# Another order of the deep slots: scores and value products side by side on TensorE

## The chip, the cores and the metric

The kernel runs on 1 core of one Trainium2 chip. The metric is the device time of one execution, in microseconds (us); lower is better. The core has five engines that the text names as the profile does: PE (TensorE matmul; PEld is its weight load), DVE (VectorE), ACT (ScalarE), POOL (GpSimd) and SP (SyncE, which issues the DMAs).

## The reference

Sixteen sequences of 256 tokens, 128 features each, float32:

```
x = x + local_attention(layernorm(x))       # first layer: 16 heads of 8, windows of 32
y = layernorm(x)
for i in range(6):                          # the deep layers
    y = attn(shift(y), Wqkv[i], ...) + y    # 16 heads of 64, windows of 32, look back one window,
                                            # q and k normalised and rotated (rope)
    y = ffn(shift(y), ...) + y              # layernorm, W1 (2 x 341), gate * gelu, W2
x = x + y
```

`shift` moves the second half of the features one token on. The queries, keys and values are products of the tokens with Wqkv (128 x 3072); softmax runs over each query's window and the one before.

## The kernel before, in words

The first layer comes first and takes about a tenth of the time; the change does not touch it. The six deep layers are 96 **instances** (layer x sequence), 16 sequences per layer. Each engine runs a written-out list of steps, its **slot**, over and over (`pe_deep_slot`, `act_deep_slot`, `dve_deep_slot`, `pool_deep_slot`, `sp_deep_slot`). Each step names the instance it works on as an offset: `pe_scores_of(e, s, b, at, 0, 1)` is score pair 1 of the instance of this slot, `pe_project_in(..., 2, 0)` projection 0 of the instance two further on. So several instances are in work at once, and one slot holds the work of one instance. The engines are bound together by semaphores alone: each step waits for the counts that its inputs and its output buffer need, and an engine never goes past a step that waits.

The steps of one instance:

- `pe_project_in` 0 to 7 (L901 to L903): Q and K, each as three bf16 products of 512 columns into one PSUM bank. ACT squares the bank (`act_square`, L1050), DVE sums the squares (`dve_sum_squares`, L1128) and applies rope (`dve_rope`, L1147 and L1148), after which the bank is free. POOL adds the two halves (`pool_rotate`, L1264) and, once the norms are refined (`dve_refine`, L1190 to L1194), scales them (`pool_scale`, L1278). PE transposes (`pe_transpose` 0 to 7, L950), ACT copies the result to q and k (`act_copy_t`, L1070).
- `pe_values_in` 0 to 3: V, the same three products; ACT copies the bank to a stage (`act_copy_v`, L1082), SP's DMAs place it.
- For each of four pairs (128 queries x 8 heads): scores (`pe_scores_of`, mask L967 and products L973, in 64 x 64 tiles of the array), `dve_max_of` (L1203), `dve_shift` (L1215), `act_exp_of` (L1092), `dve_sum_of` (L1228, L1230), `pool_normalise_of` (L1288), `pe_transpose_probs_of` (L989), `act_copy_pt_of` (L1102), the value products (`pe_values_of`, L1008, 96 x 64) and `act_copy_out` (L1114). There is one buffer for scores, one for transposed probabilities and one for outputs.
- `pe_project_out` (L1024), `dve_residual_of` (L1240).
- The FFN: `act_ff_shift` (L1385), `pe_ff_mean` (L1314), `dve_ff_centre` (L1430), `act_ff_square` (L1395), `pe_ff_variance` (L1325), `dve_ff_variance` (L1440), the seed and refine shared with Q and K, `pe_ff_rstd` (L1340), `dve_ff_norm` (L1450), `act_ff_affine` (L1405), `pe_ff_up` in three chunks (L1357), `act_ff_gelu` (L1417, after which ACT loads the exponential's table again, L1420), `dve_ff_gate` (L1462), `pe_ff_down` (L1370), `dve_ff_residual` (L1475). `dve_outer` (L1488) adds the outer residual in the last layer.

**The ring.** Projections, value projections, Q/K transposes, the output projection and the FFN's products share three PSUM banks. `WORK_RING` lists these 27 users in PE's order; the user at place j has bank j mod 3, and before it starts PE waits until the user three places before has been read (`pe_wait_bank`): for `pj` by DVE's rope, for `t` and `v` by ACT's copy, for `mu` by DVE's variance, for `rb` by the norm, for `up` by the gate, for `dn` and `out` by the residuals. Two waits that bear on the FFN and on the buffers:

```
e.wait_ge(s.ff_gated, k.c[NF] + (c - 1))                # act_ff_gelu: GELU c waits for gate c - 2
    if c == NF - 1:
        e.preload_act_table_set(EXP_SET)                # after the last GELU
```

```
e.wait_ge(s.t_full, k.c[8] + (u + 1 - 8))               # pool_rotate u: transpose u of the instance before is done
```

The weights of the next layer are split on POOL during the slots (`pool_next_weights`, six pieces in every layer but the last).

## Time and profile before

| | |
|---|---|
| median of 3 runs | 3563.55 us (3558.95 to 3563.68) |
| the profiled execution | 3559.2 us |
| its span, first to last instruction | 3557.4 us |
| granted clock of TensorE, mean | 0.997 |
| PE busy | 3480.7 us, 98% |
| PEld busy | 2617.2 us, 74% |
| DVE busy | 3220.0 us, 91% |
| ACT busy | 2739.7 us, 77% |
| POOL busy | 2580.3 us, 73% |
| share of PE in the chain that ended last | 96% |
| one slot, from an instance to the next | 33.01 us in 91 of 95 steps |

Busy time is the union of an engine's instructions over the span. The chain is followed back from the last instruction, at each step to what released it. The ends of matmuls are modelled and overlap the next matmul's start, so lengths on PE are best taken from one start to the next. In the timeline below a row is a run of like instructions on one engine: its start, its length, engine, line, operation, output and inputs, their number, and in brackets the idle time before it and what ended it.

### The profile page before, as it was taken

To read this page: it belongs to the slowest core of one execution; us is meant where nothing else is said; L and a number is where in the kernel's file an instruction comes from. 1 tells how busy PE (TensorE), PEld (TensorE's weight loads), DVE (VectorE), ACT (ScalarE), POOL (GpSimd) and SP (SyncE) were. 2 spreads that over 40 slices of the span, in tenths; PEclk is the share of its full clock that TensorE was granted. 3 is DMA by queue.
4 is the path that set the end of the run, shared out by engine and by line. 5 is a ranking of instruction groups with operands and counts; after the bars stand their busy time and mean duration, and the time that the engine had idled before them with its cause. 6 is when DMAs were issued, how large, how long until landed. Compare 5 with 4: busy or idle time off the path is not lost.

```text
span 3557.4 us, 112862 instructions
## 1 busy us (share of the span) xinstructions
PE 3480.7 (98%) x45216; PEld 2617.2 (74%) x45216; DVE 3220.0 (91%) x5488; ACT 2739.7 (77%) x4727; POOL 2580.3 (73%) x2263
## 2 busy tenths in 40 slices
PE   7998899999999999999999999999999999999998
PEld 5776577777777777777777777777777777777776
DVE  6877899999999999999999999999999999999995
ACT  4665677887887887887788788788788878878876
POOL 2433887777778777778777777877877877777772
PEclk9999999999999999999999999999999999999999
DMA  1000222122112212212212221221221221121121
GB/s 44 27 2 29 55 54 57 40 60 55 47 44 57 54 47 55 54 37 57 66 38 51 54 50 44 66 51 39 54 57 37 66 51 41 44 74 49 36 51 41
DMA packets 61573, 171.67 MB, mean 48 GB/s; under 512 B 9472, under 2 KB 21248, under 8 KB 60672
## 3 DMA queue, kind: packets, MB, share of 16 engines
q1 hardware_dynamic: 61056, 164.46, 18.1%
q8 instruction: 363, 5.95, 0.7%
q14 instruction: 154, 1.26, 0.1%
HBM read 21.82 MB, written 4.19 MB: 7 GB/s over the span
## 4 chain that ended last, share of the span: by engine, by line
PE 96%; issue 1%; DVE 1%; ACT 1%; POOL 1%; DVEq 0%; POOLq 0%; ACTq 0%
PE bank L1008 11%; PE bank L950 10%; PE bank L989 10%; PE bank L1024 9%; PE bank L1357 8%; PE bank L901 8%; PE bank L973 7%; PE bank L903 7%; PE bank L902 7%; PE bank L1370 4%; PE bank L967 3%; PE bank L370 2%; PE bank L350 2%; PE bank L1325 1%; PE bank L335 1%; PE bank L1340 1%
## 5 line engine op out<-in xcount | busy, mean ns | idle before, releaser
L1264 POOL TENSOR_TENSOR rotbuf<-mbuf 128x512 f32<-128x512 f32 x768 | 969.0, 1272 | 510.2 <-PE bank L950 321.6
L1278 POOL TENSOR_TENSOR rotbuf<-rotbuf,rs 128x512 f32<-128x512 f32 x768 | 787.0, 1045 | 66.0 <-DVE rs L1194 66.0
L1128 DVE TENSOR_REDUCE ss<-sq 128x8 f32<-128x512 f32 x768 | 516.7, 677 | 156.4 <-ACT sq L1050 156.2
L1288 POOL TENSOR_TENSOR probs<-probs,rden 128x768 f32<-128x768 f32 x384 | 564.6, 1470 | 120.9 <-DVE rden L1230 120.9
L1147 DVE TENSOR_TENSOR mbuf<-bank,table 128x512 f32<-128x512 f32 x768 | 528.5, 688 | 13.4
L1148 DVE TENSOR_TENSOR mbuf<-bank,table 128x512 f32<-128x512 f32 x768 | 523.2, 681 | 0.0
L1050 ACT ACTIVATE sq<-bank 128x512 f32<-128x512 f32 x768 | 458.9, 598 | 53.9 <-PE bank L903 21.9
L1008 PEld LDWEIGHTS bank<-probs_t,vbuf 96*64 96x64 f32 x12288 | 389.4, 138 | 144.4 <-issue 104.3
L1070 ACT ACTIVATE kbuf<-bank 128x512 f32<-128x512 f32 x384 | 217.9, 593 | 347.1 <-PE bank L950 347.1
L950 PE MATMUL bank<-ident,rotbuf 128*128 128x128 f32 x3072 | 451.9, 275 | 15.2 <-DVE mbuf L1148 8.6
L901 PE MATMUL bank<-weights,inputs 128*128 128x512 bf16 x1152 | 442.8, 384 | 10.5 <-DVE mbuf L1148 8.2
L1008 PE MATMUL bank<-probs_t,vbuf 96*64 96x64 f32 x12288 | 442.4, 225 | 1.1 <-ACT outs_t L1114 1.1
L902 PE MATMUL bank<-weights,inputs 128*128 128x512 bf16 x1152 | 438.8, 381 | 0.0
L903 PE MATMUL bank<-weights,inputs 128*128 128x512 bf16 x1152 | 438.6, 381 | 0.0
L950 PEld LDWEIGHTS bank<-ident,rotbuf 128*128 128x128 f32 x3072 | 356.7, 141 | 103.3 <-DVE mbuf L1148 60.3
L989 PE MATMUL bank<-ident,probs 128*96 128x128 f32 x3072 | 404.0, 274 | 0.6 <-ACT probs_t L1102 0.5
L1102 ACT ACTIVATE probs_t<-bank 96x1024 f32<-96x1024 f32 x384 | 390.6, 1017 | 5.0 <-PE bank L989 2.7
L1215 DVE TENSOR_TENSOR probs<-bank,row_max 128x768 f32<-128x768 f32 x384 | 366.8, 955 | 6.7
L989 PEld LDWEIGHTS bank<-ident,probs 128*96 128x96 f32 x3072 | 340.8, 129 | 38.9 <-POOL probs L1288 1.5
L1203 DVE TENSOR_REDUCE row_max<-bank 128x8 f32<-128x768 f32 x384 | 364.7, 950 | 1.3 <-PE bank L973 1.3
L1228 DVE TENSOR_REDUCE den<-probs 128x8 f32<-128x768 f32 x384 | 362.1, 943 | 0.0
L1024 PE MATMUL bank<-outs_t,weights 128*128 128x256 f32 x1536 | 347.6, 379 | 0.6 <-DVE x_stream L1475 0.6
(111 smaller groups left out, 6114.6 us busy)
## 6 DMA issues: line engine op xcount, KB each, us to landing
vbuf<-v_stage SPq DMA_DIRECT2D x192, 384.0 KB, 4.5
vbuf<-v_stage SPq DMA_DIRECT2D x192, 256.0 KB, 4.0
vbuf<-v_stage SPq DMA_DIRECT2D x96, 128.0 KB, 4.5
stage<-in_wqkv SPq DMA_DIRECT2D x36, 256.0 KB, 5.3
weights<-in_wo SPq DMA_DIRECT2D x6, 512.0 KB, 6.8
weights<-in_x_t SPq DMA_DIRECT2D x1, 2048.0 KB, 7.3
out_t<-weights SPq DMA_DIRECT2D x1, 2048.0 KB, 6.3
weights<-out_t SPq DMA_DIRECT2D x1, 2048.0 KB, 10.4
```

Of the source, the lines that this page charges most:

```text
L901: e.matmul(out, xh, wh, start=True, stop=False)
L902: e.matmul(out, xh, wl, start=False, stop=False)
L903: return e.matmul(out, xl, wh, start=False, stop=True)
L950: mm = e.transpose(work_bank(b, "t", u)[:, P * q:P * (q + 1)], b.rot[:, u, P * q:P * (q + 1)], b.ident[:, :])
L989: mm = e.transpose(b.pt[parity][0:BLOCK_K, P * j:P * (j + 1)], b.deep_probs[:, p % 2, 4 * parity + j, :], b.ident[:, :])
L1008: mm = e.matmul(b.out[r, col:col + BLOCK_Q], b.v[:, k.par, 2 * t + blk_half, DIM_HEAD * h:DIM_HEAD * (h + 1)], b.deep_ptf[:, p % 2, 512 * ...
L1024: mm = e.matmul(out, b.wo[k.layer % 2][:, chunk, :], b.ot8[:, chunk, :], start=chunk == 0, stop=chunk == INNER // P - 1)
L1147: e.tensor_tensor(b.m1[:, u % 2, :].rearrange("p (h s d) -> p h s d", h=8, s=2), pj, cos, ALU.mult)
L1148: e.tensor_tensor(b.m2[:, u % 2, :].rearrange("p (h s d) -> p h s d", h=8, s=2), pj[:, :, ::-1, :], sin, ALU.mult).then_inc(s.pj_free, 1)
L1264: e.tensor_tensor(b.rot[:, u, :], b.m1[:, u % 2, :], b.m2[:, u % 2, :], ALU.add).then_inc(s.rotated, 1)
L1278: e.tensor_tensor(v, v, r, ALU.mult).then_inc(s.scaled, 1)
L1288: e.tensor_tensor(probs, probs, b.rden[:, p % 2, :].unsqueeze(2).broadcast_to([P, 8, BLOCK_K]), ALU.mult).then_inc(s.probs, 1)
```

## The change

It writes the four engines' slots and the ring in another order; the steps themselves, their number and their waits are as they were. On PE, `pe_scores_of` and `pe_values_of` stood apart from each other in eight places of a slot. Now they stand in five: values 1 alone, scores 1 with values 2, values 3 with scores 2, scores 3 alone, values 0 with scores 0. Some steps work on another instance than before in the same slot (an offset that is one more or less), among them ff up, projection 5 and value projection 1.

```diff
--- before.py
+++ after.py
@@ -60,10 +60,10 @@
 PAIRS = 4
 WORK_BANKS = 3
 WORK_RING = (
-    ("pj", 5, 1), ("up", 0, -3), ("up", 1, -3), ("up", 2, -3), ("pj", 6, 1), ("mu", 0, -2), ("pj", 7, 1),
-    ("t", 6, 0), ("v", 1, 1), ("t", 7, 0), ("v", 2, 1), ("pj", 0, 2), ("v", 3, 1), ("pj", 1, 2),
-    ("t", 0, 1), ("t", 1, 1), ("rb", 0, -2), ("t", 2, 1), ("dn", 0, -3), ("t", 3, 1), ("pj", 2, 2),
-    ("v", 0, 2), ("pj", 3, 2), ("t", 4, 1), ("out", 0, -1), ("t", 5, 1), ("pj", 4, 2),
+    ("t", 5, 0), ("pj", 6, 1), ("mu", 0, -2), ("pj", 7, 1), ("t", 6, 0), ("t", 7, 0), ("dn", 0, -3),
+    ("v", 2, 1), ("pj", 0, 2), ("v", 3, 1), ("pj", 1, 2), ("t", 0, 1), ("t", 1, 1), ("rb", 0, -2),
+    ("t", 2, 1), ("pj", 2, 2), ("out", 0, -1), ("pj", 3, 2), ("v", 0, 2), ("t", 3, 1), ("pj", 4, 2),
+    ("t", 4, 1), ("pj", 5, 2), ("up", 0, -2), ("up", 1, -2), ("up", 2, -2), ("v", 1, 2),
 )
 PE_REACH = (-3, 2)
 ACT_REACH = (-3, 2)
@@ -1562,141 +1562,138 @@
 
 def pe_deep_slot(e, s, b, at):
 
-    pe_project_in(e, s, b, at, 1, 5)
-    pe_scores_of(e, s, b, at, 0, 0)
-    pe_ff_up(e, s, b, at, -3, 0)
-    pe_values_of(e, s, b, at, -1, 0)
-    pe_ff_up(e, s, b, at, -3, 1)
-    pe_transpose_probs_of(e, s, b, at, -1, 2)
-    pe_ff_up(e, s, b, at, -3, 2)
+    pe_transpose(e, s, b, at, 0, 5)
     pe_project_in(e, s, b, at, 1, 6)
     pe_ff_mean(e, s, b, at, -2)
     pe_values_of(e, s, b, at, -1, 1)
     pe_project_in(e, s, b, at, 1, 7)
+    pe_transpose_probs_of(e, s, b, at, -1, 3)
+    pe_ff_variance(e, s, b, at, -2)
     pe_scores_of(e, s, b, at, 0, 1)
-    pe_ff_variance(e, s, b, at, -2)
-    pe_transpose_probs_of(e, s, b, at, -1, 3)
+    pe_values_of(e, s, b, at, -1, 2)
     pe_transpose(e, s, b, at, 0, 6)
-    pe_values_in(e, s, b, at, 1, 1)
     pe_transpose(e, s, b, at, 0, 7)
+    pe_ff_down(e, s, b, at, -3)
     pe_values_in(e, s, b, at, 1, 2)
     pe_project_in(e, s, b, at, 2, 0)
-    pe_values_of(e, s, b, at, -1, 2)
     pe_values_in(e, s, b, at, 1, 3)
-    pe_scores_of(e, s, b, at, 0, 2)
     pe_project_in(e, s, b, at, 2, 1)
     pe_values_of(e, s, b, at, -1, 3)
-    pe_transpose_probs_of(e, s, b, at, 0, 0)
+    pe_scores_of(e, s, b, at, 0, 2)
     pe_transpose(e, s, b, at, 1, 0)
     pe_transpose(e, s, b, at, 1, 1)
+    pe_transpose_probs_of(e, s, b, at, 0, 0)
     pe_ff_rstd(e, s, b, at, -2)
     pe_transpose(e, s, b, at, 1, 2)
-    pe_ff_down(e, s, b, at, -3)
-    pe_transpose(e, s, b, at, 1, 3)
     pe_project_in(e, s, b, at, 2, 2)
-    pe_transpose_probs_of(e, s, b, at, 0, 1)
+    pe_project_out(e, s, b, at, -1)
+    pe_project_in(e, s, b, at, 2, 3)
     pe_scores_of(e, s, b, at, 0, 3)
     pe_values_in(e, s, b, at, 2, 0)
-    pe_project_in(e, s, b, at, 2, 3)
+    pe_transpose(e, s, b, at, 1, 3)
+    pe_transpose_probs_of(e, s, b, at, 0, 1)
+    pe_project_in(e, s, b, at, 2, 4)
     pe_transpose(e, s, b, at, 1, 4)
-    pe_project_out(e, s, b, at, -1)
-    pe_transpose(e, s, b, at, 1, 5)
-    pe_project_in(e, s, b, at, 2, 4)
+    pe_project_in(e, s, b, at, 2, 5)
+    pe_values_of(e, s, b, at, 0, 0)
+    pe_scores_of(e, s, b, at, 1, 0)
+    pe_ff_up(e, s, b, at, -2, 0)
+    pe_ff_up(e, s, b, at, -2, 1)
+    pe_ff_up(e, s, b, at, -2, 2)
+    pe_transpose_probs_of(e, s, b, at, 0, 2)
+    pe_values_in(e, s, b, at, 2, 1)
 
 
 def act_deep_slot(e, s, b, at):
 
-    act_square(e, s, b, at, 0, 6)
-    act_copy_pt_of(e, s, b, at, -2, 2)
-    act_ff_square(e, s, b, at, -3)
-    act_square(e, s, b, at, 0, 7)
-    act_exp_of(e, s, b, at, -1, 0)
-    act_copy_out(e, s, b, at, -2, 1)
-    act_copy_t(e, s, b, at, -1, 6)
-    act_copy_v(e, s, b, at, 0, 1)
-    act_copy_pt_of(e, s, b, at, -2, 3)
-    act_copy_t(e, s, b, at, -1, 7)
-    act_square(e, s, b, at, 1, 0)
-    act_seed(e, s, b, at, 0)
-    act_copy_out(e, s, b, at, -2, 2)
-    act_copy_v(e, s, b, at, 0, 2)
-    act_copy_v(e, s, b, at, 0, 3)
-    act_exp_of(e, s, b, at, -1, 1)
-    act_square(e, s, b, at, 1, 1)
+    act_copy_out(e, s, b, at, -2, 3)
     act_copy_t(e, s, b, at, 0, 0)
     act_copy_t(e, s, b, at, 0, 1)
+    act_exp_of(e, s, b, at, -1, 1)
     act_copy_pt_of(e, s, b, at, -1, 0)
     act_copy_t(e, s, b, at, 0, 2)
+    act_square(e, s, b, at, 1, 2)
+    act_exp_of(e, s, b, at, -1, 2)
+    act_input_of(e, s, b, at, 2)
+    act_square(e, s, b, at, 1, 3)
+    act_ff_affine(e, s, b, at, -3)
+    act_ff_shift(e, s, b, at, -2)
     act_copy_t(e, s, b, at, 0, 3)
-    act_square(e, s, b, at, 1, 2)
-    act_copy_out(e, s, b, at, -2, 3)
-    act_ff_affine(e, s, b, at, -3)
     act_copy_v(e, s, b, at, 1, 0)
-    act_square(e, s, b, at, 1, 3)
-    act_exp_of(e, s, b, at, -1, 2)
+    act_square(e, s, b, at, 1, 4)
+    act_copy_pt_of(e, s, b, at, -1, 1)
+    act_square(e, s, b, at, 1, 5)
+    act_copy_out(e, s, b, at, -1, 0)
+    act_copy_t(e, s, b, at, 0, 4)
     act_exp_of(e, s, b, at, -1, 3)
-    act_copy_t(e, s, b, at, 0, 4)
+    act_ff_gelu(e, s, b, at, -3, 0)
+    act_ff_gelu(e, s, b, at, -3, 1)
+    act_ff_gelu(e, s, b, at, -3, 2)
+    act_copy_v(e, s, b, at, 1, 1)
     act_copy_t(e, s, b, at, 0, 5)
-    act_square(e, s, b, at, 1, 4)
-    act_square(e, s, b, at, 1, 5)
-    act_input_of(e, s, b, at, 2)
-    act_copy_pt_of(e, s, b, at, -1, 1)
-    act_ff_gelu(e, s, b, at, -3, 0)
-    act_copy_out(e, s, b, at, -1, 0)
-    act_ff_gelu(e, s, b, at, -3, 1)
-    act_ff_shift(e, s, b, at, -2)
-    act_ff_gelu(e, s, b, at, -3, 2)
+    act_square(e, s, b, at, 1, 6)
+    act_copy_pt_of(e, s, b, at, -1, 2)
+    act_ff_square(e, s, b, at, -2)
+    act_square(e, s, b, at, 1, 7)
+    act_copy_out(e, s, b, at, -1, 1)
+    act_exp_of(e, s, b, at, 0, 0)
+    act_copy_pt_of(e, s, b, at, -1, 3)
+    act_copy_t(e, s, b, at, 0, 6)
+    act_copy_t(e, s, b, at, 0, 7)
+    act_copy_out(e, s, b, at, -1, 2)
+    act_seed(e, s, b, at, 1)
+    act_copy_v(e, s, b, at, 1, 2)
+    act_square(e, s, b, at, 2, 0)
+    act_copy_v(e, s, b, at, 1, 3)
+    act_square(e, s, b, at, 2, 1)
 
 
 def dve_deep_slot(e, s, b, at):
 
+    dve_max_of(e, s, b, at, -1, 2)
+    dve_ff_norm(e, s, b, at, -3)
+    dve_shift(e, s, b, at, -1, 2)
+    dve_sum_of(e, s, b, at, -1, 1)
+    dve_sum_squares(e, s, b, at, 1, 2)
+    dve_sum_of(e, s, b, at, -1, 2)
     dve_rope(e, s, b, at, 1, 2)
+    dve_residual_of(e, s, b, at, -2)
+    dve_sum_squares(e, s, b, at, 1, 3)
+    dve_rope(e, s, b, at, 1, 3)
     dve_max_of(e, s, b, at, -1, 3)
     dve_shift(e, s, b, at, -1, 3)
-    dve_sum_squares(e, s, b, at, 1, 3)
-    dve_rope(e, s, b, at, 1, 3)
-    dve_sum_of(e, s, b, at, -1, 2)
-    dve_residual_of(e, s, b, at, -2)
+    dve_sum_squares(e, s, b, at, 1, 4)
+    dve_rope(e, s, b, at, 1, 4)
+    dve_sum_squares(e, s, b, at, 1, 5)
+    dve_rope(e, s, b, at, 1, 5)
     dve_sum_of(e, s, b, at, -1, 3)
-    dve_sum_squares(e, s, b, at, 1, 4)
-    dve_sum_squares(e, s, b, at, 1, 5)
-    dve_rope(e, s, b, at, 1, 4)
-    dve_rope(e, s, b, at, 1, 5)
-    dve_max_of(e, s, b, at, 0, 0)
     dve_ff_gate(e, s, b, at, -3, 0)
     dve_ff_gate(e, s, b, at, -3, 1)
+    dve_ff_gate(e, s, b, at, -3, 2)
+    dve_max_of(e, s, b, at, 0, 0)
     dve_shift(e, s, b, at, 0, 0)
-    dve_ff_gate(e, s, b, at, -3, 2)
+    dve_sum_squares(e, s, b, at, 1, 6)
     dve_ff_centre(e, s, b, at, -2)
-    dve_sum_squares(e, s, b, at, 1, 6)
     dve_rope(e, s, b, at, 1, 6)
     dve_sum_squares(e, s, b, at, 1, 7)
     dve_ff_variance(e, s, b, at, -2)
     dve_rope(e, s, b, at, 1, 7)
     dve_max_of(e, s, b, at, 0, 1)
     dve_clamp(e, s, b, at, 1)
+    dve_sum_of(e, s, b, at, 0, 0)
+    dve_ff_residual(e, s, b, at, -3)
+    dve_outer(e, s, b, at, -6)
     dve_shift(e, s, b, at, 0, 1)
-    dve_sum_of(e, s, b, at, 0, 0)
+    dve_refine(e, s, b, at, 1)
     dve_sum_squares(e, s, b, at, 2, 0)
-    dve_refine(e, s, b, at, 1)
     dve_rope(e, s, b, at, 2, 0)
     dve_sum_squares(e, s, b, at, 2, 1)
     dve_rope(e, s, b, at, 2, 1)
-    dve_sum_of(e, s, b, at, 0, 1)
-    dve_ff_norm(e, s, b, at, -2)
-    dve_max_of(e, s, b, at, 0, 2)
-    dve_shift(e, s, b, at, 0, 2)
-    dve_ff_residual(e, s, b, at, -3)
-    dve_outer(e, s, b, at, -6)
-    dve_sum_squares(e, s, b, at, 2, 2)
 
 
 def pool_deep_slot(e, s, b, at):
 
-    pool_rotate(e, s, b, at, 0, 5)
     pool_scale(e, s, b, at, -1, 7)
-    pool_input_of(e, s, b, at, 1)
-    pool_next_weights(e, s, b, at(0))
     pool_rotate(e, s, b, at, 0, 6)
     pool_rotate(e, s, b, at, 0, 7)
     pool_normalise_of(e, s, b, at, -1, 0)
@@ -1704,17 +1701,20 @@
     pool_scale(e, s, b, at, 0, 1)
     pool_scale(e, s, b, at, 0, 2)
     pool_scale(e, s, b, at, 0, 3)
+    pool_rotate(e, s, b, at, 1, 0)
+    pool_rotate(e, s, b, at, 1, 1)
+    pool_next_weights(e, s, b, at(0))
+    pool_scale(e, s, b, at, 0, 4)
     pool_normalise_of(e, s, b, at, -1, 1)
-    pool_rotate(e, s, b, at, 1, 0)
-    pool_scale(e, s, b, at, 0, 4)
-    pool_scale(e, s, b, at, 0, 5)
-    pool_rotate(e, s, b, at, 1, 1)
+    pool_input_of(e, s, b, at, 2)
     pool_rotate(e, s, b, at, 1, 2)
     pool_rotate(e, s, b, at, 1, 3)
     pool_normalise_of(e, s, b, at, -1, 2)
+    pool_scale(e, s, b, at, 0, 5)
+    pool_rotate(e, s, b, at, 1, 4)
+    pool_normalise_of(e, s, b, at, -1, 3)
     pool_scale(e, s, b, at, 0, 6)
-    pool_normalise_of(e, s, b, at, -1, 3)
-    pool_rotate(e, s, b, at, 1, 4)
+    pool_rotate(e, s, b, at, 1, 5)
 
 
 def sp_deep_slot(e, s, b, at):
```

## Rows read from the trace of the kernel before

**Rows 1.** Windows: one slot; busy us (count) per engine, PE's clock, DMA

```profile
1804.76:1837.77 33.01, 32.98 (x417) 24.73 (x417) 30.79 (x53) 26.48 (x46) 25.09 (x23) 1.00 0.18 46
```

**Rows 2.** Timeline of PE: scores, up chunks, values, transposes, projection

```profile
1812.73 0.36 PE L967 MATMUL bank<-maskb,identb 64*64 64x384 bf16 x4
...
1813.68 1.13 PE L1357 MATMUL bank<-ff_xn,wffn 128*128 128x256 f32 x4
1814.74 1.15 PE L1008 MATMUL bank<-probs_t,vbuf 96*64 96x64 f32 x32
1815.82 1.13 PE L1357 MATMUL bank<-ff_xn,wffn 128*128 128x256 f32 x4
1816.79 1.04 PE L989 MATMUL bank<-ident,probs 128*96 128x128 f32 x8
1817.67 1.03 PE L1357 MATMUL bank<-ff_xn,wffn 128*85 128x256 f32 x4
1818.53 0.38 PE L901 MATMUL bank<-weights,inputs 128*128 128x512 bf16 x1
```

**Rows 3.** Timeline of PE in the last slots: scores with values behind them

```profile
3478.74 0.36 PE L967 MATMUL bank<-maskb,identb 64*64 64x384 bf16 x4
...
3479.68 1.15 PE L1008 MATMUL bank<-probs_t,vbuf 96*64 96x64 f32 x32
```

**Rows 4.** Timeline of PE: transpose 6, a value projection, transpose 7

```profile
1823.85 0.60 PE L950 MATMUL bank<-ident,rotbuf 128*128 128x128 f32 x4
1824.28 0.38 PE L901 MATMUL bank<-weights,inputs 128*128 128x512 bf16 x1
...
1824.71 0.38 PE L903 MATMUL bank<-weights,inputs 128*128 128x512 bf16 x1
1825.13 0.66 PE L950 MATMUL bank<-ident,rotbuf 128*128 128x128 f32 x4
```

**Rows 5.** Timeline of PE and DVE: a projection, its squares, pair steps

```profile
1803.15 0.38 PE L901 MATMUL bank<-weights,inputs 128*128 128x512 bf16 x1
...
1804.63 0.69 DVE L1128 TENSOR_REDUCE ss<-sq 128x8 f32<-128x512 f32 x1 [0.70 <-ACT sq L1050]
...
1806.55 0.95 DVE L1203 TENSOR_REDUCE row_max<-bank 128x8 f32<-128x768 f32 x1
...
1808.41 0.67 DVE L1128 TENSOR_REDUCE ss<-sq 128x8 f32<-128x512 f32 x1
...
1810.33 0.94 DVE L1228 TENSOR_REDUCE den<-probs 128x8 f32<-128x768 f32 x1
...
1811.42 0.37 DVE L1240 TENSOR_TENSOR x_stream<-bank,x_stream 128x256 f32<-128x256 f32 x1
```

**Rows 6.** Timeline of ACT: a table load and what follows; a GELU that waited

```profile
1819.22 1.28 ACT L1420 ACT_TABLE_LOAD   x1
1820.51 0.60 ACT L1050 ACTIVATE sq<-bank 128x512 f32<-128x512 f32 x1
...
3536.39 0.47 ACT L1417 ACTIVATE ff_ge<-bank,vecs 128x256 f32<-128x256 f32 x1 [4.11 <-PE bank L1357]
```

**Rows 7.** Timeline of POOL and DVE: rotates, a normalisation, the refine

```profile
1824.62 2.59 POOL L1264 TENSOR_TENSOR rotbuf<-mbuf 128x512 f32<-128x512 f32 x2 [4.13 <-PE bank L950]
1828.10 1.47 POOL L1288 TENSOR_TENSOR probs<-probs,rden 128x768 f32<-128x768 f32 x1 [0.90 <-DVE rden L1230]
1828.50 1.16 DVE L1190 TENSOR_TENSOR newton_a<-rs 128x66 f32<-128x66 f32 x1
...
1830.10 0.68 DVE L1147 TENSOR_TENSOR mbuf<-bank,table 128x512 f32<-128x512 f32 x1
...
3542.76 0.23 DVE L1190 TENSOR_TENSOR newton_a<-rs 128x66 f32<-128x66 f32 x1 [0.68 <-ACT rs L1179]
```

**Rows 8.** Timeline of PE: ff down and the output projection

```profile
1801.33 1.54 PE L1370 MATMUL bank<-ff_h,wffn 128*128 128x256 f32 x6
...
1807.45 3.62 PE L1024 MATMUL bank<-outs_t,weights 128*128 128x256 f32 x16
```

## The prediction

> **What bounds the kernel now.** I read the windows first, then TensorE's order of work over one slot, then the engines that hand buffers back. A slot takes 33.01 us; PE is busy for 32.98 of it at full clock, DVE for 30.79, ACT for 26.48, POOL for 25.09 [rows 1]. So PE sets the pace, and DVE has two microseconds a slot to spare. The slot repeats for 91 of the 95 steps from instance to instance. Only two things inside it can shrink: what PE loses around its tile groups, and one short wait. The wait is at the eighth Q/K transpose: a 512-column matmul is followed by the next after 0.215 us, but the last before transpose 7 by 0.42 [rows 4]. That is 0.20 us, spent on the bank of projection 7.
>
> **What a tile group costs.** In [rows 2] stand scores, up 0, values, up 1, transposes, up 2, projection. The three up chunks have the same four matmuls and take 1.06, 0.97 and 0.86. Coming after a tile group costs 0.11; standing also before one costs 0.09 more. Scores take 0.95 and values 1.08, to the start of what follows.
>
> **The seam.** The change puts scores and values side by side three times a slot. They are not the same tiles (64 by 64 against 96 by 64), so the price from one to the other could lie between nothing (the tail of the first group falls away, about 0.15) and a full leave and return (0.09 more). The old kernel happens to have the pair in its last slots: scores start at 3478.74, values at 3479.68 [rows 3]. That is 0.94, as long as scores take before full-array work (0.95). So the seam keeps the tail and saves only the entry. The other order (values, then scores) I take alike.
>
> **PE's own sum.** Eight separate tile groups become five islands: three entries go, 3 x 0.09 = 0.27. Up 1 now follows up 0 and loses its 0.11; projections and transposes that no longer follow a tile group give a few hundredths, 0.02. Together 0.40. All eight tails stay. With the 0.20 wait gone too, PE's slot would be 33.01 - 0.40 - 0.20 = 32.4. That is the gain if nothing is late, 0.6 us a slot.
>
> **What is late next.** The change also reorders the ring, so each bank's next user moves. I followed DVE and ACT through the new order from the start of projection 3 (time 0). The pieces: 1.48 from a projection's start to its sum of squares on DVE; sum of squares with rope 1.92; maximum with shift 1.86; a row sum with reciprocal 1.09 [rows 5].
> DVE, without a pause: projection 3 (1.48 + 1.92), maximum and shift of pair 3 (1.86), projections 4 and 5 (3.84), row sum 3 (1.09): 10.19. Each of these inputs is there in time, the nearest with 0.1 to spare (projection 4's squares). Then comes gate 0. Its GELU waits behind the exponential of pair 3 and a table load on ACT; I get its end at 10.3. GELU 2 cannot start before gate 0 is done, since two GELU buffers serve three chunks: 10.3 + 0.48 + 0.03 = 10.84. After it the table load starts, 0.49 later (1819.22 in [rows 6] follows such a GELU), then 1.29 until ACT does its next instruction [rows 6]. In the new order that next one is the copy of value projection 1, and its bank is what the FFN's mean matmul waits for. 10.84 + 0.49 + 1.29 + 0.60 copy + 0.06 = 13.28. PE itself arrives at 12.82 (projections 0.65, or 0.74 before a tile group, Q/K transposes 0.44, probability transposes 0.87, scores 0.95, values 1.08, up 0.97 + 0.86 + 0.86). **First new stall: 0.46.** In the old order a square followed this load, with nothing on PE behind it so soon. The first load does not wait for its matmul: at 3536.39 ACT had been idle for 4.11 us, load done, before the GELU [rows 6]; so it is not counted behind up 0.
> The Trainium skill ("ScalarE: Activation LUTs", What ACT_TABLE_LOAD costs) puts a change of set at 1283 ns for the load and 1380 ns of drain behind it, 2.66 us in all. The row has the load's 1.28 and no drain. By the page's figure two loads in this chain would add 2.75 us a slot, an estimate of some 3840 us for the whole; I go by the row.
>
> From the mean at 13.28 PE needs 5.7 to transpose 6 (mean 0.53, values 1.08, projection 0.66, transposes 0.87, variance 0.54, scores 0.95, values 1.08): 18.99. POOL's rotate 6 waits for that transpose, 0.77 after its start [rows 4, 7], 0.04 more here behind a tile group: 19.80. Two rotates (2.59 in [rows 7], the second held a little; I take 2.5) and the normalisation of pair 0 follow: it runs from 22.3 to 23.8. In that time DVE reaches the refine: ff down starts at 19.91, its matmuls take 1.54 [rows 8], residual and shift bring DVE to 22.8. And the refine's first operation does not run beside POOL's normalisation. In [rows 7] it starts 0.40 after it, takes 1.16 and ends 0.09 after it; with POOL idle the same instruction takes 0.23 (3542.76). So here it ends at 23.85, the rest takes 0.44, the first sum of squares and rope of the next instance 1.92: 26.2, and with 0.15 until PE can have the bank, 26.36. PE wants it for transpose 0 at 26.01. **Second stall: 0.35.** The next sum and rope end at 28.3, where PE wants ff rstd at 28.15: **third, 0.13.** From there to projection 3 it is 0.49 + 0.44 + 0.65 + 3.46 (the output projection, 3.62 less its overlap [rows 8]): 5.03.
>
> **The sum.** The loop closes at 28.3 + 5.0 = 33.3, against 33.01: 32.4 from PE and 0.9 of stalls. Slower by 0.27 to 0.3; I take 0.28. Over 92 full slots: 26 us. Filling and draining I cost at nothing (the same number of slots and chains), within 4. The weight splits on POOL moved behind rotate 1: 3 us in 30 slots, ahead of a normalisation that PE wants 4 us later, covered; without that cover a transpose would wait up to 0.5 in five slots. The value copies' DMAs have 5 us in hand. The profiled execution took 3559.2 (span 3557.4), 4 below the median, so 3585 there and 3589 as a median.
>
> **Rivals.**
> 1. *The refine runs clear of POOL.* The first stall stays, but DVE meets no running normalisation: 0.23 in place of 1.05, and transpose 0 and rstd have their banks in time. The slot is 13.28 + 19.55 = 32.83, a gain of 0.18, 17 us: 3547. It decides once DVE arrives more than 0.5 us earlier, or POOL's normalisation more than 1 us earlier. For: windows of that size depend on two latencies. Against: both hang on PE's transposes 6 and 7 and ff down, which follow each other. This is the way to the other side.
> 2. *PE is never kept waiting.* 32.4 a slot, 56 us less: 3508. It needs the load or the GELU off the path to the mean. Against: every step there is in program order.
> 3. *More is late than I found.* Margins of 0.1 to 0.2 stand at projection 4, up 0 and up 2; if they break, or a latency is 0.1 longer at each hand-over, the slot is 33.6: 54 us more, 3618.
> 4. *The seam is free* (different tiles side by side overlap). In the loop only one seam (scores 1, values 2) lies on PE's path, the others under DVE's: 33.15, 13 us more, 3576. Against: rows 3. The Trainium skill ("TensorEngine Tiling (Array Packing)", Key Properties) says a change of tiling mode drains the array, but not one of tile alone; whether 96-row and 64-row products are one mode decides it, and by that rule the trace's 0.94 says two.
>
> **How the numbers follow.** Forecast 0.64, rival 1 0.13, rival 2 0.07, rival 3 0.11, rival 4 0.05. The forecast's own range, 33.15 to 33.45, is 3576 to 3604. To take in rival 1 and part of rival 3 it goes from 3543 to 3606, which leaves out rival 2 and most of rival 3. A measurement of this kernel can tell some 0.2%, 7 us, from no change. Faster: rival 2 and most of rival 1, 0.18. Same: the rest of rival 1, the ends of the forecast and rival 4, 0.1. Slower: 0.72.
>
> **What would show it.** Right: a slot of 33.3 in the windows, PE's idle time before L1314 with ACT v_stage (L1082) as its releaser, about 0.4; idle before L950 and L1340 with DVE mbuf (L1148); L1190 still about 1 us and ending with a POOL L1288; up chunks 0.97, 0.86, 0.86; a seam 0.15 to 0.17 long. Wrong: L1190 at 0.23 (rival 1); no gap before the mean matmul (2); a longer slot with gaps before L901 or L1357 (3); values 0.02 behind the last score (4).

## The result, and the profile after

The kernel after takes 3616.43 us (median of 4 runs, 3614.06 to 3616.96) beside 3562.94 for the kernel before (4 runs): a ratio of 1.0151, 95% interval 1.0134 to 1.0169. It is slower by 53.5 us, where the prediction had 26. The sign was right; the time lies 10 us above the end of the range.

The profiled execution took 3616.2 us, its span 3614.4. Windows of two slots of after, columns as in [rows 1]; the second is the slot in which a piece of weights is split on POOL and the table of scales made:

```profile
1793.26:1826.76 33.50, 32.38 (x414) 25.07 (x417) 30.93 (x53) 26.53 (x46) 25.09 (x23) 1.00 0.30 76
1826.76:1860.84 34.08, 32.58 (x414) 25.08 (x417) 31.02 (x53) 26.53 (x46) 27.95 (x26) 1.00 0.18 44
```

PE is busy for less of a slot than before (32.38 against 32.98) and yet the slot is 0.49 longer: PE waits for 1.1 us. The page says the same of the whole, first by engines, then by the chain that ended last:

```profile
PE 3429.6 (95%) x44836; PEld 2654.8 (73%) x45216; DVE 3230.2 (89%) x5488; ACT 2743.3 (76%) x4727; POOL 2577.0 (71%) x2263
...
PE 63%; DVE 13%; ACT 11%; issue 11%; POOL 1%; DVEq 0%; ACTq 0%; POOLq 0%
```

PE had 96% of that chain before. What it waits for now, from the view of waits (engine, line, waited for: us in total, times, longest):

```profile
PEld bank L1314 <- ACT v_stage L1082: 91.5, 92, 1.0
PE bank L1314 <- ACT v_stage L1082: 46.1, 92, 0.5
PEld bank L950 <- DVE mbuf L1148: 54.2, 96, 2.4
PE bank L950 <- DVE mbuf L1148: 35.9, 96, 2.2
PEld bank L1340 <- DVE mbuf L1148: 18.6, 92, 0.2
```

Three waits stand in every one of the 92 full slots, in the three places that the prediction named: before the mean (L1314), before transpose 0 (L950) and before ff rstd (L1340). Their sizes are best read from starts of the timeline of PE, since matmul ends are modelled (the first matmul of a projection is missing from some records):

```profile
1805.85 2.86 PE L1357 MATMUL bank<-ff_xn,wffn 128*128 128x256 f32 x12
1808.54 1.04 PE L989 MATMUL bank<-ident,probs 128*96 128x128 f32 x8
...
1810.93 0.38 PE L903 MATMUL bank<-weights,inputs 128*128 128x512 bf16 x1
1811.81 0.70 PE L1314 MATMUL bank<-ff_xs,inv_dim 128*128 128x256 f32 x2 [0.50 <-ACT v_stage L1082]
1812.44 1.15 PE L1008 MATMUL bank<-probs_t,vbuf 96*64 96x64 f32 x32
...
1823.70 0.83 PE L973 MATMUL bank<-kbuf,qbuf 64*64 64x96 f32 x32
1824.84 1.09 PE L950 MATMUL bank<-ident,rotbuf 128*128 128x128 f32 x8 [0.30 <-DVE mbuf L1148]
1825.77 1.04 PE L989 MATMUL bank<-ident,probs 128*96 128x128 f32 x8
1826.76 0.71 PE L1340 MATMUL bank<-ident,rs 128*128 128x128 f32 x4
```

The up chunks take 2.69 us together (1805.85 to 1808.54), as forecast with 0.97 + 0.86 + 0.86. A matmul of 512 columns is followed after 0.22, but the mean matmul comes 0.88 after its predecessor: 0.66 of waiting, and the mean then takes 0.63 to the next start instead of the 0.52 that it takes where nothing held it (in a later run), so this wait costs PE 0.77. From the start of the score products (L973) to transpose 0 it is 1.14; without the wait 0.76 (later run): 0.38.

The first wait, in the timelines of ACT and DVE:

```profile
1805.02 0.60 ACT L1114 ACTIVATE outs_t<-bank 128x512 f32<-128x512 f32 x1 [0.18 <-PE bank L1008]
1805.51 0.59 ACT L1070 ACTIVATE kbuf<-bank 128x512 f32<-128x512 f32 x1
1806.13 0.85 ACT L1092 ACTIVATE probs<-probs 128x768 f32<-128x768 f32 x1
1806.99 1.28 ACT L1417 ACT_TABLE_LOAD   x1
1808.29 0.84 ACT L1417 ACTIVATE ff_ge<-bank,vecs 128x256 f32<-128x256 f32 x2
1809.38 0.47 ACT L1417 ACTIVATE ff_ge<-bank,vecs 85x256 f32<-85x256 f32 x1 [0.25 <-DVE ff_h L1462]
1809.87 1.28 ACT L1420 ACT_TABLE_LOAD   x1
1811.16 0.60 ACT L1082 ACTIVATE v_stage<-bank 128x512 f32<-128x512 f32 x1
...
1808.80 0.88 DVE L1462 SCALAR_TENSOR_TENSOR ff_h<-bank,vecs,ff_ge 128x256 f32<-128x256 f32 x2 [0.19 <-ACT ff_ge L1417]
```

This is the chain as predicted: gate, third GELU, table load, copy, mean. The load takes 1.28 and the copy begins 1.29 after its start, as in [rows 6]. The drain of 1.38 us that the Trainium skill ("ScalarE: Activation LUTs", What ACT_TABLE_LOAD costs) puts behind a load is not there in this trace either. The second wait, in the timelines of POOL and DVE:

```profile
1820.79 1.47 POOL L1288 TENSOR_TENSOR probs<-probs,rden 128x768 f32<-128x768 f32 x1
...
1819.95 0.49 DVE L1475 SCALAR_TENSOR_TENSOR x_stream<-bank,vecs,x_stream 128x256 f32<-128x256 f32 x1 [0.86 <-PE bank L1370]
1820.36 0.95 DVE L1215 TENSOR_TENSOR probs<-bank,row_max 128x768 f32<-128x768 f32 x1
1821.22 1.12 DVE L1190 TENSOR_TENSOR newton_a<-rs 128x66 f32<-128x66 f32 x1
```

L1190 starts inside POOL's normalisation and ends 0.08 after it (1822.34 against 1822.26), with 1.12 for work of 0.22.

**Where the 57.0 us of span went** (3614.4 - 3557.4), from the starts of ff rstd (L1340) in both traces: 0.49 in each of 92 steps, 45.1; 0.58 more in five of them, 2.9; 0.18 more in eight steps of the last layer, 1.4; 1.1 more in the first and the 92nd step together, which the kernel before did in 32.54 and 32.25; 0.5 in the last three steps; 4.6 ahead of the first ff rstd (452.1 against 447.5) and 1.4 behind the last. The medians differ by 3.5 less than the two spans, since the profiled execution of the kernel before was 3.7 us under its median and that of after 0.2.

### The profile page after: what moved, and what is told of

Same layout as the page of the kernel before. It is cut to its first block, busy times and chain, and to the rows that moved or that the text cites. A ratio compares the mean times of both kernels' runs of the same rounds, so it can differ in the third digit from the quotient of the medians.

```text
span 3614.4 us, 112456 instructions
## 1 busy us (share of the span) xinstructions
PE 3429.6 (95%) x44836; PEld 2654.8 (73%) x45216; DVE 3230.2 (89%) x5488; ACT 2743.3 (76%) x4727; POOL 2577.0 (71%) x2263
## 4 chain that ended last, share of the span: by engine, by line
PE 63%; DVE 13%; ACT 11%; issue 11%; POOL 1%; DVEq 0%; ACTq 0%; POOLq 0%
PE bank L950 9%; PE bank L1024 9%; PE bank L1008 8%; PE bank L989 7%; PE bank L902 4%; PE bank L1370 3%; PE bank L973 3%; PE bank L903 3%; DVE newton_a L1190 3%; DVE probs L1215 3%; PE bank L901 3%; ACT ff_ge L1417 3%; ACT L1420 2%; DVE ss L1128 2%; DVE mbuf L1148 2%
## 5 line engine op out<-in xcount | busy, mean ns | idle before, releaser
L1148 DVE TENSOR_TENSOR mbuf<-bank,table 128x512 f32<-128x512 f32 x768 | 523.1, 681 | 0.0
L950 PE MATMUL bank<-ident,rotbuf 128*128 128x128 f32 x3072 | 441.3, 276 | 37.6 <-DVE mbuf L1148 35.9
L902 PE MATMUL bank<-weights,inputs 128*128 128x512 bf16 x1152 | 439.3, 381 | 32.6 <-issue 15.1
L950 PEld LDWEIGHTS bank<-ident,rotbuf 128*128 128x128 f32 x3072 | 353.6, 141 | 119.2 <-DVE mbuf L1148 54.2
L903 PE MATMUL bank<-weights,inputs 128*128 128x512 bf16 x1152 | 439.2, 381 | 0.0
L1092 ACT ACTIVATE probs<-probs 128x768 f32<-128x768 f32 x384 | 326.1, 849 | 3.1 <-DVE probs L1215 0.8
L1024 PEld LDWEIGHTS bank<-outs_t,weights 128*128 128x128 f32 x1536 | 291.6, 190 | 49.8 <-DVE ff_xc L1450 1.7
```

Source lines behind the costliest of these rows:

```text
L902: e.matmul(out, xh, wl, start=False, stop=False)
L903: return e.matmul(out, xl, wh, start=False, stop=True)
L950: mm = e.transpose(work_bank(b, "t", u)[:, P * q:P * (q + 1)], b.rot[:, u, P * q:P * (q + 1)], b.ident[:, :])
L1024: mm = e.matmul(out, b.wo[k.layer % 2][:, chunk, :], b.ot8[:, chunk, :], start=chunk == 0, stop=chunk == INNER // P - 1)
L1148: e.tensor_tensor(b.m2[:, u % 2, :].rearrange("p (h s d) -> p h s d", h=8, s=2), pj[:, :, ::-1, :], sin, ALU.mult).then_inc(s.pj_free, 1)
```

## The experiments

Eleven kernels ran. "Slot" is the distance from one instance's ff rstd to the next in the profiled execution. A join (the prediction calls it a seam) is a place where scores and a value product stand side by side on PE. The ratios are to the kernel before, timed on the same chip (medians of 3562.0 to 3563.4), with the 95% interval behind them.

**1. The table load two places later.** Into the kernel after, on ACT; the load that ended the GELUs of an instance is now an own step:

```diff
     act_copy_v(e, s, b, at, 1, 1)
     act_copy_t(e, s, b, at, 0, 5)
+    act_load_exp(e, at(-3))
     act_square(e, s, b, at, 1, 6)
     act_copy_pt_of(e, s, b, at, -1, 2)
```

> The changed kernel with one step moved on ACT: the load of the exponential's table no longer stands right behind GELU 2 but behind the copies of value projection 1 and of transpose 5. Theory (the slot is set by a loop of three hand-overs, the first of them this load ahead of the value copy): the gap of 0.66 us before the mean matmul goes, the variance may gain some 0.2, the second wait (transpose 0 for the bank of projection 0) stays; slot 32.95 to 33.1 in place of 33.50, time 3565 to 3582. Rival (DVE or the seams set the slot, the load is only where the slack shows): the gap moves elsewhere, slot above 33.4, time above 3605.

Measured: 3629.26, ratio 1.0184 (1.0171 to 1.0198), slot 33.64. Slower than after; the expected 3565 to 3582 was missed. The timelines of ACT and PE:

```profile
1813.65 1.28 ACT L1424 ACT_TABLE_LOAD   x1
1814.94 0.60 ACT L1050 ACTIVATE sq<-bank 128x512 f32<-128x512 f32 x1
1815.43 1.01 ACT L1102 ACTIVATE probs_t<-bank 96x1024 f32<-96x1024 f32 x1
...
1813.43 0.59 PE L1314 MATMUL bank<-ff_xs,inv_dim 128*128 128x256 f32 x2
1813.95 1.15 PE L1008 MATMUL bank<-probs_t,vbuf 96*64 96x64 f32 x32
...
1816.59 1.05 PE L989 MATMUL bank<-ident,probs 128*96 128x128 f32 x8 [0.73 <-ACT probs_t L1102]
```

The mean no longer waits and takes 0.52, so the load was what it had waited for. But the copy of probability pair 2 now stands behind the load, and the transposes of pair 3 wait for it. The wait moved by three groups and grew.

**2. POOL's normalisation later.** Into after, on POOL:

```diff
-    pool_normalise_of(e, s, b, at, -1, 0)
     pool_scale(e, s, b, at, 0, 0)
     pool_scale(e, s, b, at, 0, 1)
+    pool_normalise_of(e, s, b, at, -1, 0)
     pool_scale(e, s, b, at, 0, 2)
```

> The changed kernel with one step moved on POOL: the normalisation of pair 0 stands behind scale 1 in place of ahead of scale 0, so that POOL is idle when the refine comes. Theory (the refine's first operation is held by the running normalisation, and that is what makes transpose 0 and the rstd matmul late): L1190 falls from 1.12 to about 0.23 us, the waits of 0.37 and 0.11 us before transpose 0 and rstd go, the probability transpose may wait 0.1; slot 33.0 to 33.15, time 3570 to 3583. Rival (L1190 is long by itself, or the bank wait has another cause): slot 33.4 to 33.5, time 3605 to 3620.

Measured: 3590.19, ratio 1.0078 (1.0064 to 1.0092), slot 33.12 to 33.16. L1190 is at 0.22, the waits for mbuf (L1148) before transpose 0 and before ff rstd are gone, the one before the mean remains at [0.49 <-ACT v_stage L1082]. That is rival 1 of the prediction made real, but for two things, and they are why the time lies above the expected 3570 to 3583: five slots take 34.6, 7 us together, and nine slots of the last layer 33.79, 6 us together (run 11 is on those). In the five the transposes of pair 1 wait for POOL:

```profile
1819.59 1.08 PE L989 MATMUL bank<-ident,probs 128*96 128x128 f32 x8 [1.26 <-POOL probs L1288]
```

**3. Two joins in the kernel before.** Its own order, only values 0 and 1 put beside scores 0 and 1:

```diff
     pe_scores_of(e, s, b, at, 0, 0)
+    pe_values_of(e, s, b, at, -1, 0)
     pe_ff_up(e, s, b, at, -3, 0)
-    pe_values_of(e, s, b, at, -1, 0)
...
-    pe_values_of(e, s, b, at, -1, 1)
     pe_project_in(e, s, b, at, 1, 7)
+    pe_values_of(e, s, b, at, -1, 1)
     pe_scores_of(e, s, b, at, 0, 1)
```

> The kernel before with two pairs joined on PE and nothing else moved: values 0 goes ahead of ff up 0 and so stands behind scores 0, and values 1 goes behind projection 7 and so ahead of scores 1. Theory (a seam keeps the first group's tail and saves only one entry of 0.09 us; up 1 loses its 0.11): two entries 0.18 and 0.11 make 0.3 less PE work, of which up to 0.1 may come back as a longer wait at transpose 7; slot 32.72 to 32.82, time 3535 to 3546. Rival A (seams are free, no tail): 0.3 more, slot 32.4 to 32.5. Rival B (a seam saves nothing): slot 32.9, time 3553.

Measured: 3551.78, ratio 0.9969 (0.9958 to 0.9981), slot 32.88: 0.13 less, where 0.19 to 0.29 was expected. The idea alone does pay, in the kernel whose pace PE sets. Group by group, from start to start: the three up chunks lose 0.20, the second join 0.09, the wait at transpose 7 falls by 0.11 (0.42 to 0.31 between its neighbours), and a new wait of 0.27 stands before projection 7. The view of waits names it, and the timelines of PE and DVE show it:

```profile
PEld bank L901 <- DVE ff_h L1462: 46.9, 92, 0.6
```

```profile
1813.72 0.59 PE L1314 MATMUL bank<-ff_xs,inv_dim 128*128 128x256 f32 x2
1814.42 0.39 PE L901 MATMUL bank<-weights,inputs 128*128 128x512 bf16 x1
...
1813.90 0.47 DVE L1462 SCALAR_TENSOR_TENSOR ff_h<-bank,vecs,ff_ge 85x256 f32<-85x256 f32 x1
```

Projection 7 is the third user of a work bank behind up 2, so it needs gate 2, which ends at 1814.37. The value product that used to stand ahead of it had covered that. -0.20 - 0.09 - 0.11 + 0.27 = -0.13, the slot's change.

**4. Runs 1 and 2 together.**

> The changed kernel with both moves, the table load on ACT and the normalisation on POOL. Theory (the two waits are in series in one loop, so their prices add, and behind them PE's own sum of 32.4 is the bound): slot 32.5 to 32.65, time 3525 to 3542, under both the kernel before and the changed one. Rival (another hand-over takes over as soon as both are gone, with DVE at 30.9 us of work): slot 32.9 to 33.1, time 3560 to 3580.

Measured: 3601.74, ratio 1.0111 (1.0096 to 1.0126), slot 33.27 to 33.32, 34.73 in five. Both expectations were far off. The kernel has run 1's edit in it and with it run 1's mistake: the wait for the copy of pair 2 is there again. The two edits add up, though: from run 1 to this one the slot loses 0.36 by the move on POOL, about what it lost from after to run 2 (0.38).

**5. Copy and projection earlier instead of the load later.** Into after:

```diff
+    pe_values_in(e, s, b, at, 2, 1)
     pe_transpose_probs_of(e, s, b, at, 0, 2)
-    pe_values_in(e, s, b, at, 2, 1)
...
+    act_copy_v(e, s, b, at, 1, 1)
     act_ff_gelu(e, s, b, at, -3, 2)
-    act_copy_v(e, s, b, at, 1, 1)
```

> The kernel after, with value projection 1 moved one place up on TensorE (ahead of the transposes of probability pair 2) and its copy ahead of the third GELU on ScalarE, so that the copy stands before the wait for the gate and before the second table load; both joined seams and both table loads stay. Theory (the mean waits for that copy and for nothing else, and unlike with the load moved, no later copy slips): the 0.66 us before the mean is gone, the wait before the transposes of probability pair 3 stays near zero, the waits for mbuf of 0.37 and 0.11 stay because refine is still held by POOL; slot 32.80 to 32.95 instead of 33.50, time 3552 to 3568. Rival (the slot is a closed loop through DVE in which the mean's wait is only where slack collects; another wait of the same size opens elsewhere): slot 33.3 or more, time above 3595.

Measured: 3657.36, ratio 1.0265 (1.0251 to 1.0279), slot 33.96: the rival's number, and worse than it. The mean did not wait. But PE does, twice (its timeline; the 1.51 us of the DVE row stand in that engine's):

```profile
1825.21 0.38 PE L902 MATMUL bank<-weights,inputs 128*128 128x512 bf16 x1 [0.85 <-DVE ff_h L1462]
1827.37 0.39 PE L901 MATMUL bank<-weights,inputs 128*128 128x512 bf16 x1 [0.25 <-DVE ff_h L1462]
...
1824.45 0.88 DVE L1462 SCALAR_TENSOR_TENSOR ff_h<-bank,vecs,ff_ge 128x256 f32<-128x256 f32 x2 [0.18 <-ACT ff_ge L1417]
1826.84 0.48 DVE L1462 SCALAR_TENSOR_TENSOR ff_h<-bank,vecs,ff_ge 85x256 f32<-85x256 f32 x1 [1.51 <-ACT ff_ge L1417]
```

Value projection 1 takes the bank of up 0, so it needs gate 0, which the transposes of pair 2 had covered; and GELU 2 now stands behind the copy of that late projection, so gate 2 is late as well, and with it projection 6, which takes the bank of up 2 (the row of L901). It is the mistake of run 3 again: a group moved up in a ring of three banks meets the reader of the one three places before it.

**6. The table load last**, right ahead of the exponential that needs it. Into after:

```diff
     act_square(e, s, b, at, 1, 7)
     act_copy_out(e, s, b, at, -1, 1)
+    act_load_exp(e, at(-3))
     act_exp_of(e, s, b, at, 0, 0)
     act_copy_pt_of(e, s, b, at, -1, 3)
```

> The kernel after, with the second table load moved on ScalarE to right ahead of the exponential that needs it (behind the copies of value projection 1, of transpose 5, of probability pair 2, the squares 6 and 7 and one output copy). Theory (what failed when the load was moved by two places was only that the copy of probability pair 2 then stood behind it): neither the mean nor the transposes of probability pair 3 wait for ScalarE, slot 32.80 to 33.00, time 3552 to 3572. Rival (the 1.28 us on ScalarE delay something wherever they stand: here the exponential and the copy of probability pair 3, which the last value product needs): a wait of 0.4 us or more before a value product or before scores, slot 33.3 or more, time above 3595.

Measured: 3541.7, ratio 0.9938 (0.9925 to 0.995), slot 32.73. That is 75 us less than after by moving one instruction past seven others; the number of loads is unchanged. Its window of one slot:

```profile
1759.94:1792.67 32.73, 32.11 (x414) 25.16 (x417) 30.74 (x53) 26.63 (x46) 25.11 (x23) 1.00 0.31 77
```

The slot lost 0.77, the whole price of the first wait (0.66, and 0.11 of a slower mean). The exponential and the copy behind the load are 1.3 us later, and nobody is waiting for them.

**7. Run 5 with both moves on POOL** (that of run 2, and the one shown under run 9).

> The kernel after, with value projection 1 and its copy earlier (as in the run with the copy earlier), POOL's normalisation 0 behind its scalings 0 and 1 (as in the run with the normalisation later), and the piece of the next layer's weights put on POOL where POOL has nearly 5 us idle, behind scaling 7. Theory (three separate faults of the new order: the mean's bank, refine beside POOL, the weight piece ahead of normalisation 1): all three waits gone, slot 32.35 to 32.55 in all layers but the last, no slot longer by 0.5 or more within a layer; time 3510 to 3530, faster than both kernels. Rival (with the waits gone PE or DVE runs into the next limit at the old one): slot 32.9 or more, time 3560 or more.

Measured: 3624.14, ratio 1.0169 (1.0155 to 1.0183), slot 33.59 and no longer slots. The number lies in the rival's range, but what it shows is run 5's mistake again: PE waits for gates (DVE ff_h, L1462) before the same two projections. Against run 5 the slot is 0.37 shorter by the move of the normalisation, and the five long slots are gone.

**8. One join undone in the kernel after.**

```diff
-    pe_project_in(e, s, b, at, 2, 1)
     pe_values_of(e, s, b, at, -1, 3)
+    pe_project_in(e, s, b, at, 2, 1)
     pe_scores_of(e, s, b, at, 0, 2)
```

> The kernel after, with one of its joins undone: value product 3 goes ahead of projection 1, so that it and the scores 2 no longer stand next to each other. That adds about 0.15 us of PE work in a slot, ahead of the wait of 0.37 us before transpose 0. Theory (between the mean and the rstd the new order goes at the pace of the chain through refine, so that a join there buys nothing): the wait before transpose 0 shrinks to 0.2 to 0.25, slot 33.48 to 33.54, ratio to the kernel after within 0.1%, time 3613 to 3620. Rival (each join is worth its time wherever it stands): slot 33.65, time about 3630.

Measured: 3613.12, ratio 1.0139 (1.0125 to 1.0153), slot 33.49 against 33.50. From the start of the score products (L973) to transpose 0 it is now 1.02 instead of 1.14: the wait shrank by what the join had saved. In the kernel after this join bought nothing.

**9. Load last, and POOL in order.** Run 6 with the edit of run 2, and:

```diff
     pool_scale(e, s, b, at, -1, 7)
+    pool_next_weights(e, s, b, at(0))
     pool_rotate(e, s, b, at, 0, 6)
...
-    pool_next_weights(e, s, b, at(0))
     pool_scale(e, s, b, at, 0, 4)
```

> The kernel with the load last (slot 32.73), and on POOL normalisation 0 behind the scalings 0 and 1, and the weight piece behind scaling 7, where POOL is idle. Theory (refine's hold of 0.37 and 0.11 us before transpose 0 and before the rstd is what is left, and the run with three moves gained 0.38 us in a slot by it, against the run with the copy earlier): slot 32.25 to 32.37, the slot longer by 0.58 once in a layer gone, time 3541.7 - 91 x 0.36 to 0.48 - 5 x 0.58 = 3495 to 3506. Rival (some other wait fills the freed time): slot 32.6 or more, time above 3525.

Measured: 3509.42, ratio 0.9846 (0.9833 to 0.9859), slot 32.36 in every slot up to the last layer. The slot is as expected; the time is 3 us above, since the last layer's slots became 33.03. By engines and by the chain that ended last:

```profile
PE 3398.8 (97%) x44836; PEld 2657.8 (76%) x45216; DVE 3139.4 (90%) x5488; ACT 2754.2 (79%) x4727; POOL 2570.7 (73%) x2263
...
PE 93%; issue 3%; DVE 2%; POOL 2%; ACT 1%; POOLq 0%; DVEq 0%; ACTq 0%
```

PE sets the pace again. One small wait is new: the moved normalisation ends about where the transposes of pair 0 want it, 0.17 us a slot (run 2 has it too).

```profile
PEld bank L989 <- POOL probs L1288: 30.5, 97, 0.9
```

**10. The same join undone in run 9.**

> The kernel with the load last and POOL's two moves, and value product 3 ahead of projection 1 again, so that one join is undone. In the kernel after, the same edit left the slot as it was (33.49 against 33.50). Theory (a join is worth its 0.15 us where PE does not wait behind it, and nothing where it does): here, with the wait before transpose 0 gone, the slot grows by 0.08 to 0.16 against the run with the load last and POOL's moves, time longer by 7 to 15 us. Rival (joins are worth nothing in this order at all, the transposes' input being late anyway): slot the same within 0.03, time within 3 us.

Measured: 3511.73, ratio 0.9856 (0.9843 to 0.987), slot 32.40 against 32.36. Both expectations missed, by little. PE's work from the last value projection to transpose 0 grew by 0.1 (3.42 to 3.52 from start to start), but the wait for POOL just behind it shrank by as much, from 0.17 to 0.07. The 0.04 that the slot grew stands at ff rstd, which took 0.49 instead of 0.45; why, no run shows. The run tells less than it was meant to: it gives the join's worth on PE (0.1), and not that it shows in the time; 2.3 us are within the scatter. That a join would pay in full where PE never waits behind it is therefore not shown in the new order.

**11. The outer addition last.** Run 9 with `dve_outer`, which works only in the last layer, moved from ahead of the refine to the end of DVE's slot.

> The kernel with the load last and POOL's two moves, and the addition of the outer residual (DVE, last layer only) moved from ahead of refine to the end of DVE's slot. Theory (the slots of the last layer are longer, by 0.18 us in the kernel after and by 0.67 us where refine no longer meets POOL, because this addition stands ahead of refine): these 9 slots shrink by 0.5 to 0.67 each, time shorter by 4 to 6 us than the run with the load last and POOL's moves. Rival (the last layer's slots are longer for another reason): they stay at 0.67 above the others, time the same.

Measured: 3502.4, ratio 0.9829 (0.9815 to 0.9842). The last layer's slots fell from 33.03 to 32.50 in seven of nine, one to 32.36 and one to 32.61: 4.8 us in all; the medians differ by 7. Those seven are still 0.14 longer than the others: at the end of DVE's slot the addition makes the next ff norm 0.46 later (1.11 behind ff rstd instead of 0.65), and the output projection, which takes that norm's bank three places on in the ring, comes 0.14 later. This is the fastest version: 1.7% under the kernel before and 3.2% under the kernel after, with the change's three joins in it. How much of that the joins are worth no run isolates: the new order came with them.

## Why the prediction was right or wrong

**Right: what is late next.** All three waits stood where the prediction put them, each with the releaser it named, and two runs took them away one mechanism at a time: 0.77 of the slot with the load (run 6), 0.38 with POOL's normalisation (run 2). ACT sets the pace ahead of the mean, and the refine from there to ff rstd. That the up chunks would take 0.97 + 0.86 + 0.86, that the seam would save the entry alone (scores to values 0.95, 1815.49 to 1816.44), and that L1190 would end with POOL, all held. The second wait is 0.38 (0.35 forecast); the third 0.07, with 0.10 of a slower ff rstd behind it (0.13 forecast).

**Wrong: the size of the first stall, 0.46.** Measured from the start of projection 3 (1798.34), the mean came at 13.47 and not at 13.28. PE itself would have been there at 12.81, as predicted (12.82). The failed step is the one that begins with "I get its end at 10.3" and gives GELU 2 the start 10.84. Measured, GELU 0 ended at 10.42, gate 0 started at 10.46 (1808.80) and GELU 2 at 11.04 (1809.38). Two terms were too small. ACT's exponential started 0.62 after the copy ahead of it (1805.51 to 1806.13), where I had counted 0.49, as for two instructions without a wait (a working that the prediction does not print; the next exponential in the same timeline does start 0.48 after its copy, 1814.88 to 1815.36): 0.13. And the two hand-overs round gate 0, to DVE and back, took 0.04 and 0.09, where the sum has 0.03 in all: 0.10. A slip hid 0.03 of this: 10.3 + 0.48 + 0.03 is 10.81, and the prediction went on with 10.84. Together 0.20. The load at 1.29 and the copy came as forecast, and the mean 0.65 behind the copy's start. Why the exponential was 0.13 late no run singles out.

The chain of that stretch is ACT's: its output copy waits 0.18 for value product 0 (1805.02), and from there ACT goes without a pause to GELU 1. DVE was done with its row sum at 10.27, and gate 0 waited for GELU 0, not for DVE. The first table load (1806.99) stands in this chain as well as the second; no run moves it.

From the mean on, the forecast is right to 0.05: mean to transpose 6 5.71, to transpose 0 13.03 (13.08 forecast), to rstd 14.95 (15.0), rstd to projection 3 5.08 (5.03). The 5.71 is in part luck: the mean took 0.63 and not 0.53, the variance 0.43 and not 0.54. So 0.19 a slot, 17 us, is the one error in the loop that counts. Since PE is not the bound ahead of the mean, each tenth of a hand-over goes into the slot whole.

Rival 3 had said so (0.1 more at each hand-over, 33.6, 3618). Its number came out by luck as well: the slot was 33.50, which makes 45 us and not 54, and the rest came from outside the steady slots; the gaps before L901 and L1357 that were to be its sign stand in no steady slot. A chance of 0.11 was too little all the same for a stall that was the difference of two sums of 13 us.

**Wrong: PE's own slot, 32.4.** Run 9 has 32.36 with 0.17 of waiting in it, so 32.19. With the 0.20 before transpose 7 apart, the change takes 0.62 off PE's groups and not 0.40. Three entries and up 1 account for 0.39, as forecast; the rest stands mostly at ff variance, ff down and ff rstd, which take 0.04 to 0.13 less between their new neighbours. In the kernel after this hardly counts, since the stalls absorb what PE saves (run 8).

**Wrong: "filling and draining at nothing, within 4" and "covered".** Beyond the 0.49 of each of the 92 steps the span grew by 11.9 us. Five slots with a weight piece cost 0.58 each. The prediction had named this ("up to 0.5 in five slots") and taken it as covered. It is covered in the slots whose piece has two instructions; where the third makes the table, POOL's normalisation 1 ends at 1835.11, and the transposes start at 1835.16.

```profile
1829.41 0.61 POOL L1513 CAST weights<-stage 128x512 bf16<-128x512 f32 x1
1830.10 1.16 POOL L1515 TENSOR_TENSOR weights<-stage,weights 128x512 bf16<-128x512 f32 x1
1831.40 1.27 POOL L1519 TENSOR_TENSOR table<-rope,qks 128x512 f32<-128x512 f32 x1
...
1833.64 1.47 POOL L1288 TENSOR_TENSOR probs<-probs,rden 128x768 f32<-128x768 f32 x1
...
1835.16 1.08 PE L989 MATMUL bank<-ident,probs 128*96 128x128 f32 x8 [0.37 <-POOL probs L1288]
```

Eight steps of the last layer cost 0.18 each. The outer addition was moved ahead of the refine, which the prediction did not look at. The timelines of DVE and POOL in such a slot of the kernel after:

```profile
3262.58 0.76 DVE L1488 TENSOR_TENSOR weights<-weights,x_stream 128x256 f32<-128x256 f32 x1
...
3264.12 0.62 DVE L1190 TENSOR_TENSOR newton_a<-rs 128x66 f32<-128x66 f32 x1
...
3263.00 1.66 POOL L1288 TENSOR_TENSOR probs<-probs,rden 128x768 f32<-128x768 f32 x1
```

The addition runs into POOL's normalisation, which takes 1.66 instead of 1.47, and L1190 ends with it as before (3264.74 against 3264.66), 0.18 later than in the other slots. Where the refine no longer meets POOL the whole addition counts: 0.67 in run 9, of which run 11 took 0.53 away.

The first and the 92nd step cost 1.1 more together and the last three 0.5: filling and draining were not free, since the kernel before is quicker in them than in its steady slots and the new order is not, or less so. Of the 4.6 us ahead of the first ff rstd, 2.5 are there already at the first projection of the slots (first weight load of L901 at 338.6 against 336.1), behind an opening that the change does not touch. In runs 1, 8 and 11, with that same opening, it stands at 336.8, 336.6 and 341.1. So at least half of this part is scatter between executions; what the rest is stays open, and so is the 1.4 at the end.

**The rivals.** Rival 1 (refine clear of POOL) did not happen, but run 2 made it: 33.12 where it had 32.83, 0.19 of it the size of the first stall once more, 0.1 behind the mean, where the transposes of pair 0 now wait 0.17 for the moved normalisation. Rival 4 needs no run: the seam is not free. Rival 2 (PE is never kept waiting, 3508) is what run 9 made, 3509.4, in part by chance: PE's own slot is 0.2 shorter than I had it, and 0.17 of waiting and the longer slots of the last layer fill that up.

## What to carry to other kernels

A join that saves an engine 0.1 us is worth nothing where this engine waits behind it anyway (run 8). The order with the three joins costs 1.5% as it was written; with one table load moved to right ahead of its user it gains 0.6% (run 6), and with two moves on POOL and one on DVE besides 1.7% (run 11). When an order is changed, list for each step that moves up who must have freed its buffer (in a ring of three, the reader of the group three places before), and for each long instruction without a reader (a table load) every copy queued behind it, not only the first one. And where another engine's chain sets the pace, take each hand-over from a row of the same pair of instructions; a tenth of a microsecond there is a tenth of the slot.
